# A new order for the opening of a cross-attention and quantised-FFN kernel: context, key, value, then query weights

## The reference, cut to what matters

```python
lat = layernorm(_layernorm(x), ln_l_w, ln_l_b)           # two layer norms, one after the other
ctx = layernorm(context, ln_c_w, ln_c_b)
q = (lat @ Wq)                                            # 16 heads of 64
k, v = split(ctx @ Wkv, 2)
attn = softmax(clip(einsum(q, k) * 64**-0.5, -11, 11))
x = x + (einsum(attn, v) @ Wo + bo)
x = x + ffn(_layernorm(x))                                # int8-like fake quantisation, silu gate, 1408 wide
```

## Time and profile before

| | us |
|---|---|
| median of 3 runs | 1359.35 (1358.99 to 1359.62) |
| profiled execution, its own time | 1363.62 |
| its span | 1361.9 |
| first matmul of the key products | 27.15 |
| first matmul of the value products | 62.41 |
| first matmul of group 0's scores | 99.43 |
| first `cap` of group 1 | 139.06 |

### The profile page before, as it was taken

How to read it: one execution, slowest core, us unless ns; L and a number is a source line. 1 busy time by engine, 2 the same in 40 slices (tenths; PEclk the granted TensorE clock), 3 DMA queues, 4 the chain that set the end, 5 groups by cost and what they waited for, 6 DMA issues and landing times.

```text
span 1361.9 us, 20412 instructions
## 1 busy us (share of the span) xinstructions
PE 1289.0 (95%) x7625; PEld 610.7 (45%) x7668; DVE 1166.1 (86%) x2059; ACT 787.2 (58%) x1183; POOL 409.0 (30%) x278
## 2 busy tenths in 40 slices
PE   7988999999999999999999999699999999799997
PEld 6433444544544445445444444344444444344343
DVE  6757899988988998889889857789999999789996
ACT  6557765776577557755764762233443443597671
POOL 2104424542454244424443521000000000045555
PEclk9998999999999999999999999899999999899999
DMA  7173525446246245362561335296666632299995
GB/s 286 43 220 105 128 81 158 135 124 202 74 127 216 64 148 163 109 205 59 155 219 54 115 125 131 101 284 218 204 253 254 252 104 63 93 391 423 424 400 189
DMA packets 179218, 241.72 MB, mean 177 GB/s; under 512 B 121632, under 2 KB 140848, under 8 KB 168112
## 3 DMA queue, kind: packets, MB, share of 16 engines
q1 hardware_dynamic: 179120, 240.43, 53.2%
HBM read 120.86 MB, written 90.57 MB: 155 GB/s over the span
## 4 chain that ended last, share of the span: by engine, by line
PE 71%; DVE 14%; ACT 5%; issue 4%; SPq 3%; DMA 2%; POOL 1%; POOLq 0%; DVEq 0%; ACTq 0%
PE pu L1482 10%; PE pg L1476 10%; PE pu L1510 7%; PE po L78 7%; PE po L80 7%; PE po L79 7%; PE ring L79 6%; PE ring L78 6%; PE ring L80 6%; DVE w L1448 2%; PE ring L1015 1%; ACT E L451 1%; DVE sg L1455 1%; PE ring L991 1%; SPq L1247 1%
## 5 line engine op out<-in xcount | busy, mean ns | idle before, releaser
L1351 ACT ACTIVATE sg<-pg,gate_scale 128x512 f32<-128x512 f32 x176 | 120.9, 687 | 186.9 <-PE pg L1476 186.9
L78 PE MATMUL ring<-yT,M 128*128 128x512 f16 x512 | 195.5, 382 | 0.0
L80 PE MATMUL ring<-yT,M 128*128 128x512 f16 x512 | 195.4, 382 | 0.0
L79 PE MATMUL ring<-yT,M 128*128 128x512 f16 x512 | 195.4, 382 | 0.0
L78 PE MATMUL po<-VW,p 128*128 128x512 f16 x480 | 182.8, 381 | 2.0 <-DVE p L633 2.0
L1476 PE MATMUL pg<-xqT,w 128*128 128x512 bf16 x689 | 179.5, 380 | 3.7 <-DMA xqT<-xq 2.0
L80 PE MATMUL po<-VW,p 128*128 128x512 f16 x480 | 182.7, 381 | 0.0
L79 PE MATMUL po<-VW,p 128*128 128x512 f16 x480 | 182.5, 380 | 0.0
L1482 PE MATMUL pu<-xqT,w 128*128 128x512 bf16 x690 | 179.7, 380 | 0.7
L1510 PE MATMUL pu<-w 128*128 128x512 bf16 x690 | 157.4, 386 | 19.6 <-DVE w L1450 10.1
L392 POOL TENSOR_TENSOR esum<-esum,E 128x512 f32<-128x512 f32 x96 | 131.0, 1365 | 76.3 <-ACT E L455 76.2
(11 more groups left out here) (239 smaller groups left out, 2152.4 us busy)
## 6 DMA issues: line engine op xcount, KB each, us to landing
hidden<-hb SPq DMA_DIRECT2D x11, 2816.0 KB, 9.7
hb<-hidden SPq DMA_DIRECT2D x11, 2816.0 KB, 18.4
xa<-x_rows_d SPq DMA_DIRECT2D x28, 1024.0 KB, 6.1
x<-in_x_dram SPq DMA_DIRECT2D x16, 1024.0 KB, 5.8
value_fold<-E SPq DMA_DIRECT2D x64, 256.0 KB, 2.5
VW<-value_fold SPq DMA_DIRECT2D x16, 1024.0 KB, 6.1
x_rows_d<-x SPq DMA_DIRECT2D x16, 1024.0 KB, 4.9
out_dram<-xa SPq DMA_DIRECT2D x12, 1024.0 KB, 12.7
```

The lines of the kernel that those rows point to most:

```text
L78: nc.tensor.matmul(out, a_hi, b_hi, start=first, stop=False)
L79: nc.tensor.matmul(out, a_hi, b_lo, start=False, stop=False)
L80: return nc.tensor.matmul(out, a_lo, b_hi, start=False, stop=last)
L1351: nc.scalar.activation(sg[:, n % 4], pg[n % 4][:], ACT.Silu, scale=gate_scale[:, n % FT:n % FT + 1]).then_inc(silus, 1)
```

## The change

The loads come in the order vectors, context, key, value, query weights. The squares of the query weights and the query scale move from the front of the lists into the key products (third and fourth scale swap places, so value weights have number 3 now). The eight bias columns leave the front and the first products and stand behind key products 2 to 7 and value products 0 and 1. The halves of the eight turned query blocks spread: 0 to 3 beside key products 6 and 7, 4 to 7 beside value products 0 to 3. Folding of the keys moves from value products 0 to 3 to 4 to 7, and the output weights' halves beside it. The output weights' squares and scale move forward, the bias product from behind value product 6 to behind 5. In group 0 the rows of group 1 are normalised and split beside tiles 2 to 4, 6 and 7. SyncE transposes before it stores the keys.

```diff
+    def rows_beside(s):
+        return (3, 4, 6, 7) if s == 0 else (1, 3, 5, 7)
 # SyncE
-            sp.dma_start(cx, ctx_in...).then_inc(ld_c, 16)
             for k, v in enumerate(vectors[0:4]): ...
+            sp.dma_start(cx, ctx_in...).then_inc(ld_c, 16)
-            for c in range(DC): wq32
             for c in range(DC): wk32
             for c in range(DC): wv32
+            for c in range(DC): wq32
...
-        store_kv(0)
         for t in range(TT):
             turn(0, t)
+        store_kv(0)
         sp.wait_ge(q_lo, IC)
+        sp.wait_ge(qb_ready, 1)
 # ScalarE
-        for c in range(DC):
-            square(1, wq32[:, c], c)
         for c in range(DC):
             square(0, wk32[:, c], c)
...
-            if c > 0:
-                weight_high(0, c - 1)
-        weight_high(0, DC - 1)
-        square(2, wv32[:, 0], 0)
-        kv_high(0, 0)
-        kv_high(0, 1)
-        for n in range(IC):
-            if n >= 2:
-                kv_high(0, n)
-            q_high(n)
-            if n < 3:
-                square(2, wv32[:, n + 1], n + 1)
-            if n >= 4:
-                weight_high(1, n - 4)
+            weight_high(0, c)
+        for c in range(DC):
+            square(2, wv32[:, c], c)
+            if c >= 2:
+                kv_high(0, c - 2)
+        for n in range(2, IC):
+            kv_high(0, n)
+            if n < 6:
+                weight_high(1, n - 2)
+                square(1, wq32[:, n - 2], n - 2)
+            else:
+                q_high(2 * n - 12)
+                q_high(2 * n - 11)
...
         for n in range(IC):
             kv_high(1, n)
             if n < 4:
-                fold_key(0, 2 * n)
-                fold_key(0, 2 * n + 1)
+                q_high(n + 4)
                 high_y(0, n)
-            if n in (3, 4):
-                for c in range(2 * n - 6, 2 * n - 4):
+            if n in (1, 2):
+                for c in range(2 * n - 2, 2 * n):
                     square(3, wo32 of c)
-        for k in range(DC):
-            wo_high(k)
+            if n >= 4:
+                fold_key(0, 2 * n - 8)
+                fold_key(0, 2 * n - 7)
+                wo_high(n - 4)
 # VectorE
-        rows_seen(WQ, 0)
...
-        scale_by_rows(WQ, misc[:, 0:P], 2, 3)
         norm_stats(0)
         kv_low(0, 0)
+        scale_by_sum(WV, pd[:, 0:DC], 2, 3)
         kv_low(0, 1)
-        q_low(0)
-        q_low(1)
         for n in range(2, IC):
             kv_low(0, n)
-            q_low(n)
+            if n < 6:
+                weight_low(1, n - 2)
...
+            if n == 5:
+                rows_seen(WQ, 0)
+            if n == 6:
+                scale_by_rows(WQ, misc[:, 0:P], 2, 4)
+            if n >= 6:
+                q_low(2 * n - 12)
+                q_low(2 * n - 11)
         norm_rows(0, 0)
         norm_rows(0, 1)
-        split_q_bias()
-        score_scales()
         for n in range(IC):
             kv_low(1, n)
             if n < 4:
-                fold_key(0, 2 * n)
-                fold_key(0, 2 * n + 1)
+                q_low(n + 4)
                 low_y(0, n)
...
-            if n == 5:
+            if n == 2:
+                split_q_bias()
                 rows_seen(WO, 1)
-            if n == 6:
-                scale_by_rows(WO, pd[:, 0:P], 3, 5)
-            if n == 7:
+            if n == 3:
+                scale_by_rows(WO, pd[:, 0:P], 3, 5)
+                score_scales()
+            if n >= 4:
+                fold_key(0, 2 * n - 8)
+                fold_key(0, 2 * n - 7)
+                wo_low(n - 4)
+            if n == 6:
                 dve.wait_ge(bias_rows, 1)
                 nc.vector.tensor_copy(bias_rows_sb, misc[0:H, :]).then_inc(rows_out, 1)
         score_biases()
         norm_stats(1)
...
-        for k in range(DC):
-            wo_low(k)
 # TensorE
-        for c in range(DC):
-            pe.wait_ge(ld_w[1][c], 16)
-        project_bias(0)
-        project_bias(1)
         (turn the context)
         weight_sum(0, po[1][:, 0:DC])
-        project_bias(2)
-        spread_rows(0, misc[:, 0:P], 2)
-        for n in range(3, 6):
-            project_bias(n)
         first_products()            # columns 6 and 7 stood between its chunks
+        for c in range(DC):
+            pe.wait_ge(ld_w[1][c], 16)
         turn_q(0)
         turn_q(1)
+        weight_sum(2, pd[:, 0:DC])
         for n in range(2, IC):
             product(0, n)
-            turn_q(n)
-            if n == 3:
+            if n < 4:
+                turn_q(n)
+            if n == 2:
                 pe.wait_ge(scales, 3)
-                weight_sum(2, misc[:, 0:DC])
+            project_bias(n - 2)
+            if n == 5:
+                spread_rows(0, misc[:, 0:P], 2)
+            if n == 7:
+                turn_q(4)
         for n in range(IC):
             product(1, n)
-            if n < 4:
-                fold_keys(0, n)
-            if n == 6:
+            if n < 3:
+                turn_q(n + 5)
+            if n < 2:
+                project_bias(n + 6)
+            if n == 2:
                 pe.wait_ge(qb_split, 2)
                 spread_rows(1, pd[:, 0:P], 3)
+            if n >= 4:
+                fold_keys(0, n - 4)
+            if n == 5:
                 bias_product()
-        bias_expand()
+            if n == 6:
+                bias_expand()
```

More of the change, by code:

```diff
@@ L251, in load_opening @@
         def load_opening():
-            sp.dma_start(cx, ctx_in.rearrange("b s d -> (b s) d").rearrange("(t p) d -> p t d", p=P)).then_inc(ld_c, 16)
             for k, v in enumerate(vectors[0:4]):
                 sp.dma_start(vec_rows[DC * k:DC * k + DC, :], v.rearrange("(c p) -> c p", p=P)).then_inc(ld_vec, 16)
+            sp.dma_start(cx, ctx_in.rearrange("b s d -> (b s) d").rearrange("(t p) d -> p t d", p=P)).then_inc(ld_c, 16)
             wkv_of = wkv.rearrange("(c p) (k n) -> k p c n", p=P, k=2)
             wq_of = wq.rearrange("(c p) n -> p c n", p=P)
-            for c in range(DC):
-                sp.dma_start(wq32[:, c], wq_of[:, c]).then_inc(ld_w[1][c], 16)
             for c in range(DC):
@@ L263, in load_opening @@
                 sp.dma_start(wv32[:, c], wkv_of[1][:, c]).then_inc(ld_w[2][c], 16)
+            for c in range(DC):
+                sp.dma_start(wq32[:, c], wq_of[:, c]).then_inc(ld_w[1][c], 16)
             load_x(0)
@@ L488, in weight_high @@
             if c == 0:
-                act.wait_ge(scales, (2, 4)[kind])
+                act.wait_ge(scales, (2, 3)[kind])
             if c == 0 and kind == 1:
@@ L500, in q_high @@
             if n == 0:
-                act.wait_ge(scales, 3)
+                act.wait_ge(scales, 4)
             act.wait_ge(q_turned, n + 1)
@@ L555, in on_scalar @@
                 floor(s, t)
-                if more and t % 2 == 1:
-                    high_y(s + 1, t // 2)
+                if more and t in rows_beside(s):
+                    high_y(s + 1, rows_beside(s).index(t))
                 exp(s, t)
@@ L820, in on_vector @@
             nc.vector.tensor_tensor(cT[:, 1, c, :], cf[:, c], cT[:, 0, c, :], ALU.subtract).then_inc(c_lo, 1)
-            if c > 0:
-                weight_low(0, c - 1)
-        weight_low(0, DC - 1)
-        scale_by_rows(WQ, misc[:, 0:P], 2, 3)
+            weight_low(0, c)
         norm_stats(0)
         kv_low(0, 0)
+        scale_by_sum(WV, pd[:, 0:DC], 2, 3)
         kv_low(0, 1)
-        q_low(0)
-        q_low(1)
         for n in range(2, IC):
             kv_low(0, n)
-            q_low(n)
+            if n < 6:
+                weight_low(1, n - 2)
             if n == 2:
                 norm_aggregates(0)
+            if n == 3:
                 norm_rstd(0)
-            if n == 3:
-                scale_by_sum(WV, misc[:, 0:DC], 2, 4)
-            if n >= 4:
-                weight_low(1, n - 4)
+            if n == 5:
[5 more added lines that the diff above has]
+                q_low(2 * n - 11)
         norm_rows(0, 0)
         norm_rows(0, 1)
-        split_q_bias()
-        score_scales()
         for n in range(IC):
@@ L875, in on_vector @@
                     low(s - 1, KT - 1)
-                if more and t % 2 == 0:
+                if more and t % 2 == 0 and s > 0:
                     norm_rows(s + 1, t // 2)
-                if more and t % 2 == 1:
-                    low_y(s + 1, t // 2)
+                if more and t in rows_beside(s):
+                    low_y(s + 1, rows_beside(s).index(t))
+                if s == 0 and t in (2, 3, 4, 6):
+                    norm_rows(1, (2, 3, 4, 6).index(t))
                 if s == 0 and t == 0:
@@ L1073, in first_products @@
                         ins.then_inc(kv_ready[0], 1)
-                if c < 2:
-                    project_bias(6 + c)
         def product(kind, n):
```

## The result

The changed kernel takes 1370.81 us (median of 7 runs, 1366.4 to 1372.74), the kernel before 1359.39 in the same comparison (1357.22 to 1362.74): ratio 1.0072, 95% interval 1.0059 to 1.0084, so about 9.8 us slower by the ratio (the two medians are 11.4 apart; the ratio, which comes with an interval, is what the text goes by). The forecast was 1361.0, range 1354.5 to 1367.5, with "slower" at 0.38. The direction and part of the mechanism were among its cases; the size lay outside its range. The profiled execution took 1370.81 us, its span is 1369.0, 7.1 more than before.

What follows compares the result with a forecast made beforehand. TensorE was taken to bound most of the opening, then VectorE and ScalarE up to group 1's first `cap`. Terms -3.3 + 11.6 - 6.6 = +1.7 us on 1359.35 gave 1361.0, range 1354.5 to 1367.5.

Steps and rivals of the forecast that it cites:

- Up to the value products: Opening until value product 0: front gain 9 us, partly given back; start at 59.1 for 62.41, -3.3 us.
- the walk: Hand walk through the new instruction lists with the old durations; its sums gave the predicted times, +1.7 us in all.
- the rival of dear columns: In key and value products: bias columns keep their old price, 1.65 us each; +5.9 on the sum, 1366.9, chance 0.10.
- Value products: First to last value product: 45.3 us for 33.7, with new pauses of 4.1 and 4.4 us and 3.5 for clock falls; +11.6.
- From the last value product to group 1: Last value product to group 1's first `cap`: ScalarE no longer waits for rows; 36.4 us for 43.0, -6.6.
- its case with a fallen clock: Last value product to group 1: clock falls in the 2.1 us before the scores, folds are slow; 37.7 us instead of 34.7.
- the harsh clock: Opening: clock falls in every pause, also before key product 2 and the scores; +4.7 us, 1364.1, chance 0.21.
- The kind clock: Opening: the clock does not fall in the new pauses; -5.3 us, 1354.1, chance 0.22.
- the `cap`: Sign at the opening's end: first `cap` of group 1 near 140 us.
- the case of the clock held low: Key products: bias columns hold the clock low, six products at twice 2.6 us; 1380, chance 0.05.

Runs made afterwards that it cites:

- the folds filled: Kernel with all three waits moved one step later, plus 16 unread matmuls in the 3.87 us pause between group 0's value folds: 0.9924 of the kernel before, 1350.14 us.

## Why the prediction was wrong

*Up to the value products:* predicted -3.3 us, measured -3.7 (58.74 for 62.41). Context, halves and first products came within 0.3 us of the walk (context halves 17.51 for 17.5, first key product 21.45 for 21.2), the bias column costs 0.82 at the fast level (start to start, 35.11 to 35.93), not 1.65: the rival of dear columns is out. The pause was 2.65 for 2.8, and the clock fell in it, in this execution.

*Value products:* predicted +11.6, measured +12.8 (46.3 us from first to last start for 33.5). Both pauses were right to 0.1 us. Too small was the price of the fall in the second: the expansion, too, ran slow (+0.95), and all 12 matmuls of product 7 (+2.4 for 1.75). Filling both pauses showed what the two falls cost: 4.8 us back.

*From the last value product to group 1:* predicted -6.6, measured -1.8 (41.3 from the last value start for 43.1). This is the step that failed. The walk had ScalarE done with its eighth exponential 25.8 us behind the last value product, at its own 2.15 us for a tile, and 8.9 us from there to the first `cap` of group 1; it then took 36.4, between that sum (34.7) and its case with a fallen clock (37.7). Measured, the last exponential ended 29.6 us behind the value product, 3.9 later, and the rest took 11.5 us, 2.6 longer. TensorE set the pace, not ScalarE: ScalarE waited 4.47 us for the first score, the eight tiles came at TensorE's 2.6 us, and 0.90 us for a row came on top. Then came TensorE's pause of 3.86 us between the value folds, and behind it folds, denominators (1.89 us) and the first score of group 1 ran slow; the `cap` at 146.39 waited 1.96 us for it.

The trace of before had shown both. Group 0's scores took 22.2 us there from first to last start (99.43 to 121.63) and take 22.1 now (108.72 to 130.81), so ScalarE's late rows had cost only TensorE's wait for the last tiles:

```profile
125.46 0.84 PE L1015 MATMUL ring<-w,VW 64*64 64x512 f16 x12 [2.68 <-ACT E L445]
```

This wait is gone in the changed kernel, and 0.7 us of it is lost again, as the first score of group 1 has all of its matmuls slow where before it had eight of 12 (5.2 us from its start to the `cap` for 4.5). And from the last exponential to the `cap` it was 10.8 us before, with the same slow folds and denominators; the 8.9 left them out. It needs the clock up: with the folds filled it was 8.7. My own harsh case, 37.7, had the slow folds but left out the slow first score of group 1 and the row. ScalarE's 3.8 us wait, which the term named, did go; it was worth 2.7.

-3.7 + 12.8 - 1.8 = +7.3 us, as the spans have it (+7.1). The forecast's sum, +1.7, missed 5.6 of it: 4.8 in the third term, 1.2 in the second, 0.4 the other way in the first.

The runs say +8.6 and +9.8 us. The profiled execution of before (1363.62) was slower than any of the 7 runs in its comparison, and the mechanism is at hand: the same pause makes the clock fall in some executions only, which cost 1.7 to 3.3 us each time. That this closes the last 2 us was not measured.

*The rivals:* the harsh clock (1364.1, at 0.21) came nearest, and half of it came true. The clock did fall before the scores, but not behind the first products' late chunks: key product 2 ran at 0.22 between matmuls in both profiled executions. So its +4.7 holds 1.75 us that did not come, and it is still 6.7 us too low against the median, for the reasons above. The kind clock is out for the two pauses above 4 us, behind which the changed kernel's clock fell in both profiled executions; behind 2.65 us both were seen. Most of the prediction's own signs came as it said (key product 2 at 32.08, the three pauses, the price of a column); the two that failed are the last value product, 9.1 us later and not 3 to 8, and the `cap`.

Two slips in it touch no term of the sum: ScalarE's second wait for a row was 0.88 us before, not 1.3, and the case of the clock held low adds up to about 1382, not 1380.

## What to carry over

An engine that works in order must not ask for an operand whose last producer runs behind the very product that it has just issued: three such waits, each curable by moving one line by one product, turned a 9 us gain into a 9 us loss. Charge a pause of TensorE with its length and with what may run slow behind it (0.43 us for 0.22 between matmuls of 512 columns, 2.07 for 1.12 for the fp32 expansion), and carry that through to the next engine. And when a part of a change is credited with a gain because an engine stops waiting, check who ends the stage next: look in the trace of before at how long the other engine stood for it (2.7 us here), not at how long the waiting engine did (3.8).

## What the runs showed of the hardware

A pause of TensorE of 1.74 to 1.77 us in the same code left the granted clock at 1.00 in some executions and took it to 0.57 over the next 8 us in others: four of the 14 profiled executions have slow matmuls behind it. Behind the pause of 2.65 us it fell in six of the seven executions that have it, behind 3.27 us in two of three, and behind pauses of 4.1 and 4.3 us each of the twelve times. The length alone doesn't decide: one of 1.36 to 1.39 us, a group earlier, had slow matmuls behind it in 12 of the 14; the pauses of 0.8 and 1.0 us around the expansion had them in the three kernels with both; 1.50 us had none in three. What else decides was not tested. So a single profile may be several us off the median of the runs. Matmuls whose result nobody reads keep the clock up: 35 of them, in about 7.6 us that TensorE had idled, made the kernel 4.2 us faster.
